# From QKV to attention: six first maxima computed in the first two pairs, the first half turned one product earlier, an activation table, two loads and a wait moved

## The reference, cut to what matters

```python
def _L1_cond_ref(hidden, w, ..., Wqkv, bqkv, Wp, bp, ..., num_heads):
    B, N, D = hidden.shape
    hd = D // num_heads
    h = _sln(hidden, w, ln_g, ln_b, Wg, bg, Wb, bb)
    qkv = (h @ Wqkv.T + bqkv).reshape(B, N, num_heads, hd, 3)
    q = jnp.moveaxis(qkv[..., 0], 2, 1)
    k = jnp.moveaxis(qkv[..., 1], 2, 1)
    v = jnp.moveaxis(qkv[..., 2], 2, 1)
    energy = jnp.einsum('bhqd,bhkd->bhqk', q, k)
    att = jax.nn.softmax(energy, axis=-1) / D ** 0.5
    out = jnp.einsum('bhqk,bhkd->bhqd', att, v)
    out = jnp.moveaxis(out, 1, 2).reshape(B, N, D)
    out = out @ Wp.T + bp
    h1 = out + hidden
    h2 = _sln(h1, w, ln_g, ln_b, Wg, bg, Wb, bb)
    return h2 + h1
```

## Time and profile before

| what | value |
| --- | --- |
| median of three runs | 1867.25 us (1859.41 to 1867.28) |
| profiled execution, own time | 1867.83 us |
| its span, first to last instruction | 1865.7 us |
| mean granted clock of TensorE | 0.989 |
| PE busy | 97% of the span |
| last product of the QKV stage, first of attention | 901.1 us, 903.52 us |
| attention, first to last product | 903.5 to 1756 us |

### The profile page before, as it was taken

One profiled execution on the slowest core, in us unless ns is written; L12 is line 12 of the kernel. 1 busy time (PEld: TensorE's weight loads), 2 busy tenths in 40 slices (PEclk: granted clock), 3 DMA queues, 4 the chain that ended last, 5 costly groups with the idle time before them and its releaser, 6 DMA issues. The chain is left out here.

```text
span 1865.7 us, 27084 instructions
## 1 busy us (share of the span) xinstructions
PE 1815.0 (97%) x9510; PEld 1214.0 (65%) x9510; DVE 1252.1 (67%) x1986; ACT 836.4 (45%) x1547; POOL 1217.5 (65%) x681
## 2 busy tenths in 40 slices
PE   8999999999999999999999999999999999999897
PEld 4678888888888788888555545554555555454376
DVE  4655655655655565556887777777777777777387
ACT  3223123122223122221476666666666666666465
POOL 2665465465464243332588888888988888898565
PEclk9999999999999999999999999999999999999999
DMA  7410110210103657595877778777878787865796
GB/s 271 118 35 23 57 34 22 56 34 22 56 1 118 209 206 244 180 292 181 199 164 175 184 167 184 175 181 177 182 179 185 172 182 170 185 153 133 232 383 235
DMA packets 135373, 287.10 MB, mean 154 GB/s; under 512 B 23984, under 2 KB 41520, under 8 KB 127200
## 3 DMA queue, kind: packets, MB, share of 16 engines
q1 hardware_dynamic: 102996, 200.10, 35.8%
q0 software_dynamic: 9264, 66.11, 17.4%
q10 hardware_dynamic: 23008, 19.54, 3.3%
HBM read 134.68 MB, written 84.19 MB: 117 GB/s over the span
## 5 line engine op out<-in xcount | busy, mean ns | idle before, releaser
L1619 DVE TENSOR_REDUCE at_mrow<-banks 128x1 f32<-128x512 f32 x976 | 594.1, 681 | 163.7 <-PE banks L1465 163.6
L1715 POOL TENSOR_TENSOR at_sums<-at_probs 128x2048 f32<-128x2048 f32 x127 | 596.6, 4698 | 91.5 <-DMA at_sums<-at_sums 80.2
L1599 ACT ACTIVATE at_probs<-banks 128x512 f32<-128x512 f32 x1024 | 519.7, 621 | 182.7 <-PE banks L1483 177.4
L1465 PE MATMUL banks<-early_ks,early_qs 96*128 96x512 f32 x976 | 407.9, 418 | 11.0 <-DVE at_mrow L1619 7.1
L1483 PE MATMUL banks<-early_qs,early_ks 98*128 98x512 f32 x1024 | 408.0, 417 | 1.8 <-ACT at_probs L1599 1.8
L1465 PEld LDWEIGHTS banks<-early_ks,early_qs 96*128 96x128 f32 x976 | 184.8, 189 | 145.1 <-DVE at_mrow L1619 91.6
L1483 PEld LDWEIGHTS banks<-early_qs,early_ks 98*128 98x128 f32 x1024 | 193.7, 190 | 105.6 <-ACT at_probs L1599 81.5
L1495 PE MATMUL banks<-at_probs,at_v 128*32 128x512 f32 x2048 | 249.1, 603 | 0.7 <-DMA at_v<-v_scratch 0.7
L66 PE MATMUL banks<-l_nt,l_weights 128*128 128x512 f32 x768 | 179.4, 394 | 5.4 <-DVEq L1193 4.3
L66 PE MATMUL banks<-l_ht,l_weights 128*128 128x512 f32 x768 | 178.9, 393 | 1.9 <-issue 1.9
L657 ACT ACTIVATE l_gt<-banks,mod 128x512 f32<-128x512 f32 x60 | 45.1, 778 | 299.3 <-PE banks L526 263.5
(11 more groups left out here) (147 smaller groups left out, 2155.3 us busy)
## 6 DMA issues: line engine op xcount, KB each, us to landing
at_sums<-at_sums POOLq DMA_DIRECT2D x63, 1024.0 KB, 8.3
qk_scratch<-qk_out SPq DMA_DIRECT2D x64, 512.0 KB, 6.1
early_ks<-qk_scratch SPq DMA_DIRECT2D x48, 512.0 KB, 5.2
early_qs<-qk_scratch SPq DMA_DIRECT2D x96, 256.0 KB, 5.7
attn_scratch<-at_out SPq DMA_DIRECT2D x32, 512.0 KB, 7.5
o_a<-attn_scratch SPq DMA_DIRECT2D x32, 512.0 KB, 14.5
chunk_in<-x SPq DMA_DIRECT2D x8, 1024.0 KB, 5.4
v_scratch<-qk_v ACTq DMA_DIRECT2D x32, 256.0 KB, 3.0
```

What stands on the lines that cost most here:

```text
L1465: pe.matmul(em[n % 3][:], qs[0:96, slot, half, j, c * P:(c + 1) * P], ks[0:96, slot, j, keys * CH:(keys + 1) * CH], start=True, stop=True) ...
L1599: nc.scalar.activation(probs[:, i % 4, j, :], et[n % 3][:], ACT.Exp).then_inc(exp_done, 1)
L1619: nc.vector.tensor_reduce(mrow[:, half, keys, u:u + 1], em[n % 3][:], AX.X, ALU.max).then_inc(max_done, 1)
L1715: nc.gpsimd.tensor_tensor(into, probs[:, a], probs[:, a + 1], ALU.add).then_inc(pair_ready, 1)
```

## The change

It does seven things. (1) `FIRST_MAXIMA` is 42, so the QKV stage ends behind the last V product without maxima; 22 instead of 16 maxima of group 0 are computed in its pairs 0 and 1, 11 in each: 8 in `FRONT` as ever, 3 behind the V products of the pair. (2) The first half is turned and negated behind the second V product (t = 1), not the third. (3) PE makes four matmuls more (`WARM`) before the barrier, into a bank that nobody reads. (4) ACT takes one exponential of one column (`exp_warm`) ahead of the last store of V, which loads the table there. (5) ACT no longer waits for the stores of V before the barrier; SP waits for them later, before it loads V of group 2. (6) SP issues the six query loads of group 1 ahead of the wait for the negated maxima, and so ahead of the two writes of those. (7) ACT loads `wp_raw` in group 0 behind the exponentials of block 8 (pair 4), no longer first of all.

```diff
-FIRST_MAXIMA = 8 * LEAD
+FIRST_MAXIMA = 8 * LEAD - 6
...
             sp.wait_ge(qk_done, NM * NCH)
             load_stack_keys(sp, sh, sh.early_ks, 1, 0)
+            for half in range(QH):
+                load_stack_queries(sp, sh, sh.early_qs, 1, 0, half)
             sp.wait_ge(sh.negt_taken, 1)
             for part in range(2):
...
-            for half in range(QH):
-                load_stack_queries(sp, sh, sh.early_qs, 1, 0, half)
...
-                    if last and t == TT - 2:
+                    if last and t == TT - 3:
                         turn_first(s)
                 if last:
-                    for n in maxima:
-                        maximum(s, n)
+
+                    pe.wait_ge(v_ready, TT * s + 1)
+                    for _ in range(WARM):
+                        pe.matmul(ps[KT][:], w[:, HI, 2, 0, 0:P], w[:, HI, 2, 0, :], start=True, stop=True)
...
                 for t in range(TT):
+                    if b_next is None and t == TT - 1:
+                        nc.scalar.activation(exp_warm[:], sh.eps[:, 0, 0:1], ACT.Exp)
                     store(t)
...
-            act.wait_ge(v_free, 16 * TT * (NCH + 1))
...
-                    if loads is None and t == TT - 2:
+                    if loads is None and t == TT - 3:
                         negate_first()
-                if loads is None:
-                    for n in maxima:
-                        take_maximum(n)
...
-            return [(whose, at, (n + a) // UNITS, (n + a) % UNITS, keys) for a in range(4) for keys in range(2)]
+            products = [(whose, at, (n + a) // UNITS, (n + a) % UNITS, keys) for a in range(4) for keys in range(2)]
+            if g == 0 and p < SWITCH:
+
+                rest = [(g, slot, *first_max(n)) for n in range(FIRST_MAXIMA, 4 * UNITS)]
+                products = rest[:len(rest) // 2] if p == 0 else rest[len(rest) // 2:]
+            return products
...
                 if part == 3:
+                    if g == 2:
+
+                        sp.wait_ge(sh.v_free, 16 * TT * (NCH + 1))
                     load_v(g, slot)
...
                     av(g, slot, 2 * p + 1)
+                    for product in products:
+                        max_unit(*product)
...
+                    if first and i == KC:
+                        act.dma_start(wp_raw[:], wp_t.rearrange("(k p) n -> p k n", p=P)).then_inc(wp_loaded, 16)
...
-            act.dma_start(wp_raw[:], wp_t.rearrange("(k p) n -> p k n", p=P)).then_inc(wp_loaded, 16)
```

More of the change, by code:

```diff
@@ L918, in qkv_stage @@
         NM = 2 * KT
+        WARM = 4
         w = sh.w0[:, :, 0:3].rearrange("p a c (k n) -> p a c k n", k=KT)
@@ L932, in qkv_stage @@
         rstd = sb("qk_rstd", [P, TT])
+        exp_warm = sb("qk_exp_warm", [P, 1])
         x_loaded = [sem("qk_x_loaded0"), sem("qk_x_loaded1")]
@@ L945, in qkv_stage @@
         v_done, v_ready = sem("qk_v_done"), sem("qk_v_ready")
-        v_free = sem("qk_v_free")
+        v_free = sh.v_free
         ps = sh.ps
@@ L1941, in build @@
         sh.eps = sb("eps", [P, 2, TT])
+        sh.v_free = ctx.enter_context(nc.semaphore("qk_v_free"))
         sh.e_done, sh.max_done, sh.mrow_turned, sh.maxima_joined, sh.negt_hi, sh.negt_taken, sh.negm_loaded = (
```

## The result

| | median | range | runs |
| --- | --- | --- | --- |
| before | 1864.41 us | 1859.41 to 1867.28 | 22 |
| changed | 1869.39 us | 1865.56 to 1878.88 | 22 |

The ratio is 1.0033, 95% interval [1.0025, 1.0041]: 6.2 us slower (4.7 to 7.6). The three runs of before shown ahead of the prediction lay high; with 22 the median is 2.8 us lower. The profiled execution after took 1868.61 us, span 1866.5.

What follows compares the result with a forecast made beforehand. PE was taken to bound attention wherever nothing stalls it. Terms 0.9 + 1.4 + 0.5 - 0.4 + 0.5 = +2.9 us on the profiled 1867.83 gave 1870.7, less 0.6 for the median: 1870, range 1860 to 1876.

Steps and rivals of the forecast that it cites:

- Who holds the barrier: End of the QKV stage: DVE's last six reduces end latest; barrier alone would let PE start 2.6 us earlier.
- The rows behind the queries: SP's queue before attention: negated maxima wait behind query loads, so PE starts at 904.4, +0.9 us (-0.4 to +2.0).
- Rows in time: Rival at the start of attention: rows land early, PE starts at 900.9, time 1866.4 us; chance 0.25.
- Wait for V and table: Pair 0: the 0.67 us wait for V's load goes, the moved table load is worth 0; -0.4 us.
- Six maxima: Pairs 0 and 1: six more products cost PE +1.4 us, and DVE falling behind adds 0.5 us.
- the backlog of DVE: Pairs 0 and 1: DVE falls behind PE's three added maxima, taken as 0.5 us, bounds 0 and 2.2.
- `wp_raw`: Load issued in pair 4 beside the second quad's adding DMA: +0.5 us, bounds 0 and +4.8.
- collision: Rival in the second quad: `wp_raw` delays the adding chain by 4.8 us; 1874.4 us, 1876 with clock dip; chance 0.12.
- the 2 us named as its sign: PE near 945: a wait of over 2 us for `at_sums` would show `wp_raw` delaying the adding chain.
- Its gaps within two quads: Attention: with mean DMA share 0.79, the 4.8 us of `wp_raw` transfers find gaps within two quads.
- Drift: Rival anywhere: a shifted start redraws stalls where DMAs meet, 1860 to 1876 us; by more than 3 us, chance 0.13.
- Whatever lets PE start attention earlier is thus kept to the end: All of attention: PE is the bound wherever nothing stalls it, so an earlier start lasts; no size given.

Runs made afterwards that it cites:

- e11: Kernel before with only the six maxima moved into pairs 0 and 1: ratio 1.0033, median 1869.79 us.
- e2: Changed kernel with SP writing the two rows of negated maxima ahead of the six query loads: ratio 1.0031.
- e4: Kernel before with only the load of `wp_raw` made late, behind block 8 of group 0: ratio 1.0018, median 1868.20 us.
- e9: Changed kernel with the negated rows written from POOL's empty queue instead of SP's: a single run, 1865.25 us.
- e1: Changed kernel with `wp_raw` loaded first of all in attention again: ratio 1.0014, median 1865.47 us.
- e3: Changed kernel with the negated rows written ahead of the query loads and `wp_raw` loaded at the start of attention: ratio 1.0014.
- e12: Changed kernel, rows first, queries behind V's loads, `wp_raw` behind block 2, the six maxima in pair 0 (three ahead of its V product), four matmuls kept: 1863.47 us, 0.9997.
- e5: Changed kernel with the negated rows written from ACT's queue, behind two stores of V: a single run, 1870.57 us.
- e10: Changed kernel, rows first, queries behind V's loads, `wp_raw` behind block 2, six maxima in pair 0 (three ahead of its V product), no four matmuls: 1861.38 us, 0.9995.
- e7: Changed kernel with rows first, query loads behind V's two loads, `wp_raw` behind block 2, without the four matmuls: 1862.32 us, ratio 0.9993.

## Why the prediction was right, and what in it was wrong

The time, 1870, and the sign were right: 1869.39 was measured. The size was not: +2.9 forecast, +6.2 measured (+5.0 by medians). That the time came out to within 1 us was luck: the three runs of before lay 2.8 us high, and this made up for the cost that was missed. By its steps:

- *Who holds the barrier:* that DVE's last six reduces are "the latest of the five engines" was a misreading. V's last store, for which ACT waits, landed at 902.9, 0.5 us behind DVE, and e11 shows that the six maxima alone move the barrier by 0.1 us. The sum was spared, as the change takes ACT's wait away too.

- *The rows behind the queries:* the mechanism was right. The first product came at 904.17 (forecast 904.4), released by the DMA of `at_neg_t`, as the rule of the Trainium skill (DMA: Bandwidth & Descriptors, Queues, rings and completion order) had it: issued behind the queries, the rows took 9.5 us, ahead of them 3.4 (e2). Only "can't overtake" went too far, since the first row landed 0.4 us ahead of the last query load. The term was +0.9 and measured -0.3: the last V product itself was 0.9 us later in that trace, and the last query load landed at 903.7 and not 904.3. Of the 0.9 us, 0.7 is there at the first V sum of the chunk, before anything in the stage differs. The other 0.2 is a cost that the forecast put at nothing: from the first to the last V sum it takes 10.9 to 11.0 us in each of the eleven kernels with the turn one product earlier, and 10.7 to 10.8 in before, e4 and e11. "Rows in time" gave 0.9 us under before. e2, where they are in time, was 5.8 us over, because it also puts the queries close ahead of V's load. e9, which leaves the queries early, gained 2.6 us at the mark, so the rows' wait did cost the changed kernel that much in the traces.
- *Wait for V and table:* -0.4 forecast, -0.7 measured. Pair 0 ran at 1.2 GHz as said, and no exponential stood behind a table load. In this trace the exponential behind the moved load started 0.02 us after it, so again no drain was seen.
- *Six maxima:* 1.4 + 0.5 = +1.9 forecast, +3.6 measured. The step that failed is the backlog of DVE, put at 0.5 with bounds 0 and 2.2: it was 2.2. The 1.08 us that DVE idles ahead of a pair's maxima do not help, for the three added ones come just there and use them up (DVE ran 11 reduces on end, 6.67 us).
- *`wp_raw`:* +0.5 forecast, +3.5 measured (e1; 3.4 in e4, 3.2 between e2 and e3). This was the largest error of size: 4.8 us was the bound, and the chain of adding DMAs, at 13.5 us against PE's 13.3 by my own count, left nothing to absorb it. The rival called a collision was what happened, at 0.7 of its price, though PE's wait was 1.62 us and not the 2 us named as its sign. "Its gaps within two quads", a mean share of 0.79, was a bad reason: it's the adding DMA of that very moment that mattered.

Sum of the measured terms: -0.3 - 0.7 + 3.6 + 3.5 = 6.1, or 6.3 with the 0.2 us above, against 6.2 by time. The last term has an error of over 2 us and the trace of the changed kernel shows 2.9, so the close agreement is partly luck too. Drift is not needed to explain it. That what is lost at the start is kept holds for every comparison within its interval: marks of +2.7 (e1), +3.2 (e3) and +4.7 (e11) came out as +2.6, +2.6 and +6.1 us. A gain is not kept as fully: -2.9 in e12 came out as -0.6 (interval -3.2 to +1.9), and in its trace 1.6 us of it are gone by pair 3 of group 1. "Whatever lets PE start attention earlier is thus kept to the end" holds only as long as the adding chain keeps up.

Forecasts of experiments failed too: that e2 would gain 2 to 3 us, that two terms would add in e3, that e5 would tell the queue from the engines, that e12 would gain over e10, and the size of e11, put at 2 to 3.5 us and measured at 6.1 (3.9 to 8.4).

## What to carry to other kernels

Before an engine at a barrier is relieved, list what every other engine and queue still has to bring, landings of DMAs included. Here DVE's six reduces and the store for which ACT waits ended 0.5 us apart, with the rows and V's load behind them, so e11 moved nothing and e2 only passed the wait on. Loads that are needed last go last in their queue: with the same queries behind V instead of ahead of it (and `wp_raw` behind block 2) pair 2 came 2 us earlier. A 1 MB load cost some 3.5 us of its estimated 4.8 beside a periodic DMA whose chain has as long a period as PE's own work. And an earlier start is worth only what the next chain with the same period lets through.

## What the runs showed of the hardware

Two queues did not share the DMA engines by bytes. From 889.2 to 901.0 in the changed kernel's trace SP's queue moved 2.50 MB in 1052 packets and ACT's 0.33 MB in 667. With nine loads in SP's queue the first two 256 KB stores on ACT's took 10.5 to 12.5 us to land (changed kernel, e1, e5, e9), against 7.8 and 4.4 before. And behind a stall of PE of 1.79 us the granted clock was 0.50 over 902 to 904 in one trace (e10) and stayed at 1.00 in another (e7), with the same program up to there.
